# Edge terms of a graph kernel's gather stage: one product of 99 columns per tile, with the three parts added on VectorE

## The reference

```python
x = _layernorm(x + L0(x, norm, w1, w2, src, dst, rel_type))   # messages by relation, summed by dst
x = _layernorm(x + L1(x, edge_weight1, src, dst))             # softmax over each dst's edges
x = _layernorm(x + L2(src, dst, x))                           # two steps of normalised sums
x = _layernorm(x + L3(x, src, dst, edge_attr, distances, ...))
```

```python
# L0
h1 = relu(einsum('ni,rij->nrj', inputs, weight1) + bias1)
h2 = einsum('nrj,rjo->nro', h1, weight2)
agg = segment_sum(h2[src, rel_type] * norm, dst)
# L3, for each edge
ei = emb[atom_z[src]]
ej = emb[atom_z[dst]]
adapt_logit = sum(ei * (ej @ adaptW.T), axis=-1)
mj = node_mult[dst]
```

## Time and profile before

| | us |
|---|---|
| median of 3 runs | 6427.56 |
| lowest, highest | 6416.88, 6429.94 |
| profiled execution, its own time | 6438.38 |
| its span in the trace | 6436.4 |
| gather stage in the trace | 188 to 2722 |

### The profile page before, as it was taken

One profiled execution on the slowest core, in us unless ns is written; L12 is line 12 of the kernel. 1 busy time (PEld: TensorE's weight loads), 2 busy tenths in 40 slices (PEclk: granted clock), 3 DMA queues, 4 the chain that ended last, 5 costly groups with the idle time before them and its releaser, 6 DMA issues.

```text
span 6436.4 us, 120599 instructions
## 1 busy us (share of the span) xinstructions
PE 3747.3 (58%) x46034; PEld 3072.5 (48%) x46035; DVE 4031.9 (63%) x7214; ACT 2396.8 (37%) x5124; POOL 4009.8 (62%) x4023
## 2 busy tenths in 40 slices
PE   8255555454555555434555565555565565898885
PEld 7244444332333333223544455445454455887775
DVE  5443444455555555635667666776676766888999
ACT  2111111111111111113444444444444445788886
POOL 3766666666666666675555665566666665436996
PEclk7555555555555555555666665666666567999998
DMA  4545422222222222212333333333333333687775
GB/s 161 177 156 161 131 49 48 47 57 46 49 48 47 48 49 50 42 33 54 61 60 65 62 62 61 62 64 65 60 63 63 63 63 71 190 231 196 212 213 141
DMA packets 1135498, 576.24 MB, mean 90 GB/s; under 512 B 752611, under 2 KB 1074543, under 8 KB 1134785
## 3 DMA queue, kind: packets, MB, share of 16 engines
q1 hardware_dynamic: 1030017, 457.40, 29.9%
q0 software_dynamic: 104896, 110.96, 7.9%
HBM read 399.84 MB, written 168.16 MB: 88 GB/s over the span
## 4 chain that ended last, share of the span: by engine, by line
another core or an unknown queue 23%; PE 20%; issue 19%; DVE 15%; ACT 10%; POOL 10%; SPq 3%; DMA 1%; DVEq 0%; ACTq 0%; POOLq 0%
PE ps L1388 4%; ACT rb L1772 3%; PE ps L1616 3%; DVE ps L2309 2%; POOL meta_b L1184 2%; POOL meta_b L1181 2%; PE ps L1427 2%; ACT rb L1817 2%; ACT at_table L1817 2%; PE ps L1348 1%; PE ps L1376 1%; DVE row_src L2440 1%; ACT meta_a L1698 1%; DVE row_src L2439 1%
## 5 line engine op out<-in xcount | busy, mean ns | idle before, releaser
L1058 POOL DMA_INDIRECT by_src<-meta_a,row_src x1612 | 1626.6, 1009 | 1055.0 <-issue 475.5
L1046 POOL DMA_INDIRECT ring<-h_table,meta_b x1616 | 1646.9, 1019 | 915.5 <-issue 450.2
L1683 ACT ACTIVATE ring<-ring,meta_b 128x48 f32<-128x48 f32 x1616 | 386.3, 322 | 2141.9 <-DMA ring<-h_table,meta_b 2096.1
L1388 PE MATMUL ps<-ring,WX 128*128 128x48 bf16 x2188 | 439.5, 236 | 537.5 <-DVE row_src L2440 336.3
L1427 PE MATMUL ps<-meta_a,w1T 104*112 104x256 f32 x806 | 428.0, 627 | 501.4 <-DMA meta_a<-in_attrT 225.5
L2804 DVE TENSOR_TENSOR meta_b<-big,ps 128x1152 bf16<-128x1152 bf16 (+1 forms) x546 | 698.7, 1280 | 0.0
L1570 PE MATMUL ps<-dst_i,meta_b 128*128 128x128 bf16 x2450 | 362.1, 285 | 536.6 <-ACT rb L1817 214.6
L1388 PE MATMUL ps<-row_src,WX 128*128 128x48 bf16 x4376 | 499.1, 234 | 272.7 <-issue 271.6
L1388 PEld LDWEIGHTS ps<-ring,WX 128*128 128x128 bf16 x2188 | 359.8, 164 | 558.7 <-DVE row_src L2440 347.5
L1522 PE MATMUL ps<-WX,meta_b 128*128 128x49 bf16 (+1 forms) x14742 | 575.1, 197 | 56.1 <-issue 42.1
L1388 PEld LDWEIGHTS ps<-row_src,WX 128*128 128x128 bf16 x4376 | 440.1, 166 | 314.2 <-issue 312.9
(11 more groups left out here) (388 smaller groups left out, 9012.7 us busy)
## 6 DMA issues: line engine op xcount, KB each, us to landing
by_src<-default SPq DMA_DIRECT2D x44, 1456.0 KB
meta_a<-by_src SPq DMA_DIRECT2D x229, 234.0 KB, 3.8
rb<-lo_rows SPq DMA_DIRECT2D x202, 256.0 KB
rb<-src_rows SPq DMA_DIRECT2D x273, 144.0 KB
rb<-dst_rows SPq DMA_DIRECT2D x273, 144.0 KB
meta_a<-in_attrT SPq DMA_DIRECT2D x402, 80.0 KB
ring<-h_table,meta_b POOLq DMA_INDIRECT x1616
by_src<-meta_a,row_src POOLq DMA_INDIRECT x1612
```

What stands on the lines that cost most here:

```text
L1046: pool.indirect_dma_start(ring[:, gg % RING, j, 0:width], None, table, bass.IndirectOffsetOnAxis(ap=index(g * GROUP + j), axis=0)) \
L1058: pool.indirect_dma_start(by_src, bass.IndirectOffsetOnAxis(ap=row_src[:, t:t + 1], axis=0), rec[:, q % RECS, j, :], None).then_inc(s_sc[q ...
L1388: mm = pe.matmul(acc_of(FROM[T] + h, FEAT), hot_w[:, g % 2, h, :, j], rows, start=False, stop=False, skip_group_check=True)
L1683: scaled = act.activation(row, row, ACT.Copy, scale=meta_b[:, t, M_NORM:M_NORM + 1])
```

## The change

In the fixed form `wide_terms` takes the place of `edge_terms`: one product of 99 columns for each tile and bucket, so that the three parts stand side by side in PSUM. Eight tiles of 99 words don't fit into one bank: the first five (`HEAD`) go to bank 7, the other three to a bank that is lent. Up to group 109 that is bank 4, whose sums haven't begun; from group 110 (`SWITCH`) on it is bank 0, whose sums are finished. VectorE copies bank 0's ten sums into SBUF before (`keep_bank_0`); TensorE zeroes bank 4 at group 110 and bank 0 after the last group, and VectorE copies the sums back (`put_back_bank_0`). `adapt_wide` takes the place of `adapt_group`: two reductions add the three parts into `terms_t` in SBUF and signal `s_ejr`; the copy of `mj` and the product read `terms_t` instead of the bank; the wait for the gather stands ahead of the product, and the last sum waits for the product through `s_prodt`.

```diff
+HEAD = BANK // EJ_W
+SWITCH = 110
+KEPT_A = 4
+KEPT_B = PER_BANK - KEPT_A
+BANK_0_BY = max(t for t in range(TILES_IN) if FROM[t] < PER_BANK) // GROUP + 1
...
+        terms_t = free[:, 4148:4148 + GROUP * EJ].rearrange("p (j w) -> p j w", j=GROUP)
+        kept_b = free[:, 4440:4440 + KEPT_B * FEAT].rearrange("p (s w) -> p s w", w=FEAT)
...
+        def terms_bank(g):
+            return 4 if g < SWITCH else 0
...
+            def wide_terms(g):
+                def terms(i):
+                    pe.wait_ge(s_ohe, g + 1)
+                    if g >= 1:
+                        pe.wait_ge(s_ejr, g)
+                    if g == SWITCH:
+                        pe.wait_ge(s_kept, KEPT)
+                        pe.matmul(bank(4, BANK), zeros_b[:, 0:P], zeros_b[:, :], start=True, stop=False,
+                                  skip_group_check=True)
+                    for j, T in enumerate(tiles_of(g)):
+                        to = bank(7, EJ_W, at=j * EJ_W) if j < HEAD else bank(terms_bank(g), EJ_W, at=(j - HEAD) * EJ_W)
+                        for h in range(WIDE[T]):
+                            at = (FROM[T] + h) * EJ_W
+                            mm = pe.matmul(to, ohT_e[:, g % 2, h, j * P:(j + 1) * P], ej_p[:, at:at + EJ_W],
+                                           start=(h == 0), stop=(h == WIDE[T] - 1), skip_group_check=True)
+                    mm.then_inc(s_ej, 1)
+                return terms
...
-                        sum_fixed(g, edge_terms(g))
+                        sum_fixed(g, wide_terms(g))
...
+                if fixed:
+                    pe.wait_ge(s_ejr, GROUPS_IN)
+                    pe.matmul(bank(0, BANK), zeros_b[:, 0:P], zeros_b[:, :], start=True, stop=False,
+                              skip_group_check=True).then_inc(s_kept, 1)
...
+            def adapt_wide(g):
+                ts = tiles_of(g)
+                n = len(ts)
+                parts = lambda b, m: bank(b, m * EJ_W).rearrange("p (j k w) -> p j w k", j=m, k=PARTS)
+                dve.wait_ge(s_ej, g + 1)
+                if g >= 1:
+                    dve.wait_ge(s_adapt, g)
+                if n > HEAD:
+                    dve.tensor_reduce(terms_t[:, HEAD:n, :], parts(terms_bank(g), n - HEAD), AX_X, ALU.add)
+                dve.tensor_reduce(terms_t[:, 0:min(n, HEAD), :], parts(7, min(n, HEAD)), AX_X, ALU.add).then_inc(s_ejr, 1)
+                dve.wait_ge(s_ejr, g + 1)
+                dve.tensor_copy(mj_t[:, ts[0]:ts[0] + n], terms_t[:, 0:n, EMB])
+                dve.wait_ge(s_gat[g % RING], 16 * GROUP * (g // RING + 1))
+                dve.tensor_tensor(prod_t[:, 0:n, :], terms_t[:, 0:n, 0:EMB], ring[:, g % RING, 0:n, FEAT:H2W], ALU.mult) \
+                    .then_inc(s_prodt, 1)
+                dve.wait_ge(s_prodt, PRODT + g + 1)
+                dve.tensor_reduce(adapt_t[:, ts[0]:ts[0] + n], prod_t[:, 0:n, :], AX_X, ALU.add).then_inc(s_adapt, 1)
+
+            bank_0 = bank(0, PER_BANK * ACC_W).rearrange("p (s w) -> p s w", w=ACC_W)[:, :, 0:FEAT]
+
+            def keep_bank_0():
+                dve.wait_ge(s_used, 2 * BANK_0_BY)
+                dve.tensor_copy(kept[:, :, :], bank_0[:, 0:KEPT_A, :])
+                dve.tensor_copy(kept_b, bank_0[:, KEPT_A:PER_BANK, :]).then_inc(s_kept, 1)
+
+            def put_back_bank_0():
+                dve.wait_ge(s_kept, ZEROED)
+                dve.tensor_copy(bank_0[:, 0:KEPT_A, :], kept[:, :, :])
+                dve.tensor_copy(bank_0[:, KEPT_A:PER_BANK, :], kept_b).then_inc(s_kept, 1)
+                dve.wait_ge(s_kept, BACK)
...
-                    adapt_group(g)
+                    adapt_of(g)
+                    if g == BANK_0_BY and adapt_of is adapt_wide:
+                        keep_bank_0()
...
-                first_layer(fixed_group)
+                first_layer(fixed_group, adapt_wide)
+                put_back_bank_0()
```

More of the change, by code:

```diff
@@ L95 @@
 ICH = TILES_IN // 4
+HEAD = BANK // EJ_W
[3 more added lines that the diff above has]
+BANK_0_BY = max(t for t in range(TILES_IN) if FROM[t] < PER_BANK) // GROUP + 1
+BANK_4_FROM = min(t for t in range(TILES_IN) if FROM[t] + WIDE[t] > 4 * PER_BANK) // GROUP
+assert BANK_0_BY + 2 < SWITCH < BANK_4_FROM and GROUP - HEAD <= HEAD
 NOWHERE = 255
@@ L159, in build @@
         order_mark = sb("order_mark", [P, 1])
+        kept = sb("kept", [P, KEPT_A, FEAT])
         gamma = sb("gamma", [P, FEAT])
@@ L273, in build @@
         adapt_t = free[:, 4736:4736 + TILES_IN]
+        terms_t = free[:, 4148:4148 + GROUP * EJ].rearrange("p (j w) -> p j w", j=GROUP)
+        kept_b = free[:, 4440:4440 + KEPT_B * FEAT].rearrange("p (s w) -> p s w", w=FEAT)
+        assert 4148 + GROUP * EJ <= 4440 and 4440 + KEPT_B * FEAT <= 4736
         prod_t = free[:, 6352:6352 + GROUP * EMB].rearrange("p (j w) -> p j w", j=GROUP)
@@ L436, in build @@
         s_bp = s_recl[2]
+        s_prodt, PRODT = s_embp, 2
+        s_kept, KEPT, ZEROED, BACK = s_embs, 2, 3, 4
         block = ctx.enter_context(nc.Block())
@@ L2442, in fixed_group, with first_layer @@
                     place_hots(g + 1)
-            def first_layer(weights_of):
+            def first_layer(weights_of, adapt_of):
                 early = [split(src_i, lo_src, link)]
@@ L2483, in _ @@
             with dve.If(dve.value_load(form[0:1, 0:1], min_val=0, max_val=1)):
-                first_layer(edge_group)
+                first_layer(edge_group, adapt_group)
             counts, chain[0] = chain[0], counts
             with dve.If(dve.value_load(form[0:1, 1:2], min_val=0, max_val=1)):
-                first_layer(fixed_group)
+                first_layer(fixed_group, adapt_wide)
+                put_back_bank_0()
             assert chain[0] == counts
```

## The result

Beside each other the kernel before took 6422.22 us (6413.13 to 6429.94) and the changed one 6374.73 us (6372.25 to 6381.25). The ratio is 0.9935, with a 95% interval of 0.9912 to 0.9958: 47 us or 0.65% faster. The time fell as forecast and lies in the wide range (6180 to 6440); the gain is a third of the forecast 150 us. In later sets of runs the same two kernels stood at 5447 and 5467 us, and there the change is 0.35% slower.

The account below looks back on a forecast made before the run. It took GpSimd's gather chain as the bound, with 449 us of waits on late TensorE and VectorE signals. 137 + 21 − 6 = 152, taken as 150, gave 6278 us from 6428; own range 6220 to 6350, 8 in 10 6180 to 6440.

Parts of the forecast that it names:

- What bounds the kernel: Gather stage, 2534 us, is GpSimd's chain: 2078 us its own, 449 us waits; TensorE's 15517 pairs at 0.17 us fill it.
- The price of a wide product: Edge terms on TensorE under gathers: 0.21 us per 99-column pair against 0.18 us for a narrow one.
- slower rival: Edge terms: a 99-column product completes as late as three narrow ones; 115 us slower, 6543 us; chance 0.14.
- 40 × (2.80 − 1.73) = 43 us: Gathers' 40 waits for VectorE's last reduction, L2388, shrink from 2.80 to 1.73 us each, 43 us.
- 94 + 21 = 115: Gathers' waits: 94 us off the 57 for TensorE's sums, 21 us from 12 short "remote" waits going.
- third kind: GpSimd's 84 "remote" waits, 1.73 us each: released by a late signal with nothing else to wait for.
- the floor: Gather stage: short waits are TensorE's backlog too; half of 449 us gone gives 6200 us, all 5985; chance 0.11.
- 137 + 21: Gathers' waits: 137 us off those for the sums and L2388, 21 us off the short ones.
- VectorE's cover: Adapt step: 1.12 us of sums a group hidden in VectorE's 1256 us idle; if not, 109 us in 97 groups.
- eaten by VectorE: Waits shrink 137 us but the sums cost 109 us in 97 groups: −22 us, 6406 us; chance 0.16.
- 6 us for the lent banks: Bank 0 copies, zeroing products and last hand-over: 6 us added, between 0 and 10.
- Two SBUF inputs: VectorE's product shutting out GpSimd's SBUF reads could add 83 us, making 150 into 67; left out of the sum.

Follow-up runs that it names:

- i1: Kernel before with one 33-column product of the edge terms a group instead of 24 to 48, 6300 pairs fewer: 6236 us, 0.981 against before at 6346 us.
- e2: Changed kernel without VectorE's two sums, 2188 products of 99 columns and lent banks kept: 6372 us, 0.9897 against the kernel before at 6435 us.
- e3: Kernel before with only the high part of the edge terms, 2188 products of 33 columns instead of 6564: 6365 us, 0.9896 against before.
- e4: Kernel before with all 6564 products made 99 columns wide, VectorE as before: 6443 us, 1.0013 against before.
- e1: Kernel before with VectorE's two sums over three parts added in every full group, results unused: 6478 us, 1.0065 against before at 6435 us.
- i3: Kernel before with VectorE's two sums added, the same edit in another set: 6377 us, 1.0041 against before at 6346 us.
- h2: Changed kernel without its two sums, the product reading bank 7, run at the lower level: 1.0006 against the kernel before.

## Why the prediction was right and wrong

*What bounds the kernel* held. GpSimd's own work, busy and "issue", takes 2089 to 2127 us over the whole execution in every trace with full gathers, and the differences in time within a set are its waits or its gathers' durations, to some 15 us. That its waits hang on TensorE's late signals held too: by the semaphore records three quarters of them before (337 of 449 us) are for the sums' signal, and with prompt signals all of them are gone. What didn't hold is that the pairs are a load on TensorE as long as the stage (15517 at 0.17 us): i1 is rid of 6300 of them and is 110 us faster, and at the lower level all of them fit into a stage of 2100 us with no "issue" idle on L1376.

*The price of a wide product* held. At 0.21 us against 0.18 it should have made no difference, and e2 and e3 differ by 0.01%. The slower rival (delay by columns) fell with e4. The reason given for 0.21, that 48 columns cost no more than 33 "in the sequence above", has no row: the 33 and the 48 of that sequence are numbers of products. The signal, too, came out near: 3.5 us earlier by the forecast, 2.5 us in the mean and 3.2 us at the median by the records. The single releases, 0.19 and 0.16 us a pair, gave a price that is right within half (2.3 to 2.9 us for 21.7 pairs in the three kernels with 2188, 0.11 to 0.13 us each). That was in part luck: of the 134 releases in the trace of before for which L2367 waits over 0.5 us, a quarter come within 5.0 us of the first product and a quarter after more than 10.4.

The rule of the Trainium skill ("TensorE: Matmul & The Clock Gate", section "Wait — 56ns, not 53.3ns?") gives 2188 products of 99 columns and 6564 of 33 the same shown time. The traces agree at the lower level (219 and 224 us busy) and roughly at the upper one (236 and 274 us). It doesn't speak of their worth: by it alone no pair would count, and 4376 of them counted for 1%.

*The step that failed* is in the sum over the waits: the term 40 × (2.80 − 1.73) = 43 us, by which the waits for L2388 were to shrink because TensorE's signal comes earlier. They grew, from 112 us in 40 waits to 180 us in 58, 68 us more. These 111 us are the whole difference between the forecast 158 us of waits and the measured 49. With the products alone the waits for L2388 didn't shrink either: 128 us in e3, 153 us in e2. The sums alone brought them to 237 us in e1. The waits for the sums' signal fell by 117 us, where the forecast had 94 + 21 = 115; but that is in part luck. The products alone gave 89 us (e3) and 108 us (e2), and the sums alone gave 86 us (e1), because GpSimd was then held by L2388 meanwhile. The forecast shortened the two kinds of wait each by itself, though GpSimd waits for the later of the two signals. And it took "remote" for a third kind, with nothing else to wait for; it is the sums' signal. The rival called the floor had the same gap: the semaphore records do tie those waits to TensorE, but they grew from 145 to 195 us instead of going.

The term "137 + 21" measured 63 to 70 us (e2, e3). At the signal a removed pair returned 0.11 to 0.13 us, in the time of the kernel 0.014 to 0.016 us.

*VectorE's cover* was costed at nothing in the forecast and at 109 us if it failed. The sums cost 42 us (e1), 31 us in a second set (i3). The 1256 us of idle time were real, but idle time that ends with a late signal covers work only ahead of the signal; the sums stand behind it, in line to `s_adapt`. The case "eaten by VectorE" (6406 us) came nearest: it had the sign of each part, with both too large. Products and sums measured apart give −63 + 42 = −21 us; together they gave −47. The difference is about the width of the intervals. One cause that no run tests: e1's sums delay `s_ejr`, which the product signals there, while in the changed kernel the second sum signals it. The 6 us for the lent banks were not measured apart either; e2, which lends them, is 7 us slower than e3, which doesn't, within the noise.

*Two SBUF inputs* were left out of the sum on the strength of one gather of 0.94 us beside L2440. At the upper level they can't be told from the rest. At the lower level they are 10 to 13 of a 19 us loss. One row that shows no delay isn't the mean of 202: in the same trace of before, 68 of the 202 L2440 end 0.16 us before the end of a lengthened gather, and these gathers are 23 us longer in all.

*One level.* The forecast had no case in which the signals are prompt. Nothing in the trace of before pointed to one; what it could have said is that the whole gain hung on a lateness that no row explained.

## What to carry to other kernels

When an engine waits for the later of several signals, work out when each comes, not only which one the profile names: the waits for one fell by 117 us here, and those for the other rose by 68. Ask of a release that the profile ties to nothing which semaphore changed; here it was a signal already in the list. Cover is idle time ahead of the signal that others wait for, not idle time of the engine. And where the gain hangs on a delay that no row accounts for, price the change with and without it: this one is worth −0.65% with it and +0.35% without.

## What the runs showed of the hardware

- The same program ran at 6346 to 6435 us in some sets and at 5447 to 5457 us in others. In the gather stage the durations of products, the median gather (947 ns) and the granted clock (0.50) are the same. The difference there is in when TensorE's signals come while GpSimd issues indirect DMAs: `s_ej` changes 3.5 us against 14 ns after the last product's end at the median, and L2367's idle time is 687 against 3 us. The traces of the upper level hold half as many changes of semaphores (52 against 103 thousand). The cause is open.
- At the upper level, removing load-and-product pairs brought the signal of the terms forward by 0.11 to 0.13 us each and shortened the time by about 16 ns each; 33 or 99 columns made no difference above 0.13%. At the lower level 4376 fewer pairs brought nothing (h2, 1.0006).
- A gather of 128 rows takes GpSimd 947 ns at the median, and 0.30 us pass before the next. One of 16 rows takes 853 ns.
- A VectorE product of 256 elements with both inputs in SBUF, under way as a gather starts, makes the gather last 1184 to 1190 instead of 945 ns. With one input in a bank the gather lasts 945 to 947 ns; where the product ends 0.5 us or more into the gather, the gather lasts 945 ns.
